# One ring of five PSUM banks for attention and state space model, in place of a ring of three and a ring of two

## The reference

```python
h = layernorm(x) * (1 + ca) + sa
# layer 0, mixer: causal attention and a selective state space model beside each other
xn   = ln(h)
attn = softmax(mask(q @ k.T)) @ v @ o_w          # 16 heads of 8 channels
xz   = xn @ in_proj_w;  x_c = silu(conv4(x_ssm)) # 256 inner channels
dt   = softplus(x_dbc[..., :8] @ dt_w + dt_b)
h_n  = exp(dt * A_n) * h_n + (x_c * dt) * B_n    # n = 0..15, a scan over 512 tokens
y    = sum_n C_n * h_n
ssm  = ((y + x_c * D) * silu(z)) @ ssm_out_w
x1   = h + a * attn + (1 - a) * ssm;  x1 = x1 + gelu(ln(x1) @ w1) @ w2
x    = x + ga * x1
x    = x + gb * moe(layernorm(x) * (1 + cb) + sb)          # 8 experts and a shared one
x    = x + ga1 * band_attention(...)                        # layer 1
x    = x + gb1 * gated_mlp(...)
```

## Time and profile before

| | |
|---|---|
| median of three runs | 1875.94 us (1873.93 to 1879.81) |
| the profiled execution | 1875.14 us |
| its span, first to last instruction | 1873.3 us |
| mean granted TensorE clock | 0.895 |
| busy share of the span | PE 80%, PEld 50%, DVE 72%, ACT 57%, POOL 45% |

### The profile page before, as it was taken

How to read it: one execution, slowest core, us unless ns; L and a number is a source line. 1 busy time by engine, 2 the same in 40 slices (tenths; PEclk the granted TensorE clock), 3 DMA queues, 4 the chain that set the end, 5 groups by cost and what they waited for, 6 DMA issues and landing times. The chain is left out here.

```text
span 1873.3 us, 22056 instructions
## 1 busy us (share of the span) xinstructions
PE 1506.9 (80%) x7196; PEld 935.3 (50%) x7196; DVE 1345.0 (72%) x2025; ACT 1066.2 (57%) x1776; POOL 846.7 (45%) x866
## 2 busy tenths in 40 slices
PE   4757777777777868777776788979999999988778
PEld 3334433434344344343443355558778787844673
DVE  2377868868778687786889167577868686848866
ACT  2555555555555554655555467567787878832107
POOL 3263646656555465554665431112222222336853
PEclk8877898988979989889899989889999999966889
DMA  3121212102122021121210021001111111100001
GB/s 80 51 71 46 65 44 71 57 28 76 54 65 64 27 70 55 45 69 40 67 62 18 1 90 52 24 17 43 45 40 45 40 45 40 51 1 1 1 1 45
DMA packets 61654, 84.72 MB, mean 45 GB/s; under 512 B 6588, under 2 KB 32038, under 8 KB 61542
## 3 DMA queue, kind: packets, MB, share of 16 engines
q1 hardware_dynamic: 61442, 83.30, 14.7%
q10 hardware_dynamic: 100, 0.03, 0.0%
HBM read 74.38 MB, written 8.78 MB: 44 GB/s over the span
## 5 line engine op out<-in xcount | busy, mean ns | idle before, releaser
L1002 PE MATMUL bank<-QK 127*128 127x128 bf16 (+7 forms) x1024 | 252.3, 331 | 126.1 <-DVE Mx L1268 115.1
L1710 POOL TENSOR_TENSOR dBx<-dtx,Bb 128x512 f32<-128x512 f32 x256 | 320.2, 1274 | 5.8 <-DVE hy L1284 5.8
L1317 DVE TENSOR_TENSOR hl<-lsq,hh 128x512 fp32r<-128x512 f32 x320 | 260.9, 826 | 84.2 <-ACT hh L1594 76.2
L1531 ACT ACTIVATE PT<-bank 128x512 f32<-128x512 f32 x320 | 188.2, 595 | 204.8 <-PE bank L1002 203.9
L1284 DVE TENSOR_TENSOR_SCAN hy<-bank,dBx 128x512 f32<-128x512 f32 x256 | 298.1, 1205 | 4.7 <-POOL dBx L1710 4.3
L1268 DVE TENSOR_REDUCE Mx<-bank 128x1 f32<-128x384 f32 (+3 forms) x352 | 217.6, 630 | 88.9 <-PE bank L1002 88.3
L1591 ACT ACTIVATE lsq<-bank,vcol 128x512 f32<-128x512 f32 x320 | 219.1, 693 | 108.0 <-DVE hl L1317 63.2
L1690 POOL TENSOR_SCALAR_AFFINE_SELECT PT<-PT 128x256 f32<-128x256 f32 (+1 forms) x320 | 118.2, 375 | 302.6 <-ACT PT L1531 301.2
L1729 POOL TENSOR_TENSOR stage<-stage,lrs 128x512 f32<-128x512 f32 x64 | 91.7, 1433 | 311.2 <-DVE lrs L1397 311.2
L1002 PEld LDWEIGHTS bank<-QK 127*128 127x128 bf16 (+1 forms) x1024 | 94.3, 106 | 273.3 <-DVE Mx L1268 178.8
L1002 PE MATMUL bank<-x,we1h 128*128 128x512 f32 x640 | 210.8, 411 | 18.8 <-DVE x L1305 9.4
(11 more groups left out here) (255 smaller groups left out, 2475.3 us busy)
## 6 DMA issues: line engine op xcount, KB each, us to landing
Bb<-b_dram SPq DMA_DIRECT2D x128, 256.0 KB, 3.7
stage<-w_rows SPq DMA_DIRECT2D x64, 256.0 KB, 3.2
parts<-part SPq DMA_DIRECT2D x16, 384.0 KB, 2.8
QK<-parts SPq DMA_DIRECT2D x64, 96.0 KB
QK<-parts SPq DMA_DIRECT2D x64, 64.0 KB
stage<-in_L_ffn_We_dram SPq DMA_DIRECT2D x16, 256.0 KB, 3.4
hy<-in_L_attn_x_dram SPq DMA_DIRECT2D x8, 256.0 KB, 5.6
QK<-parts SPq DMA_DIRECT2D x64, 32.0 KB
```

The source lines that it names most:

```text
L1002: return engine.matmul(o, l, r, start=start, stop=stop, tile_position=pos, skip_group_check=True)
L1317: engine.tensor_tensor(hl[:, sl, :], full[:, f, :], hh[:, sl, :].bitcast(F32), ALU.subtract).then_inc(sems["dve_hl"], 1)
L1531: engine.activation(PT[:, it["sl"], :], o[:], ACT.Exp).then_inc(sems["act_exp"], 1)
L1710: engine.tensor_tensor(dBx[:, sl, h], dtx[:, b % 2, h], Bb[:, sl], ALU.mult).then_inc(sems["pool_dbx"], 1)
```

## The change

Attention and state space model take their banks from one ring of five, 0, 1, 2, 6 and 7, each step the next in turn whichever of the two it belongs to. So every step waits for the fifth step before it in the common order to give its bank back. `take2` is gone, and its callers (`branches` for `bx` and `bz`, `steps_of` for `dbc` and `dt`, `accumulate`, `finish` for `yt` and `so`, `taps`) call `take`. While the first norms run, which use banks 0 to 5, the ring is set to 6 and 7 alone. Banks 3, 4 and 5, the order of the steps, and every instruction with its operands' shapes stay as they are; only which bank is written, and so which event is waited for.

```diff
-    ring, ring2 = [0, 1, 2], [0]
+    ring = [0, 1, 2, 6, 7]
...
-    def take2():
-        ring2[0] += 1
-        return 6 + (ring2[0] - 1) % 2
...
-            k = take2()
+            k = take()
             it = step("bx", b=b, h=h, bank=k, free=free.get(f"b{k}"), ready=r_n[b], xc_free=free.get(f"xc{s}"))
...
-            k = take2()
+            k = take()
             it = step("bz", b=b, h=h, bank=k, free=free.get(f"b{k}"), zg_free=free.get(f"zg{s}"))
...
-        k, k2 = take2(), take2()
+        k, k2 = take(), take()
         it = step("dbc", b=b, bank=k, bank2=k2, free=free.get(f"b{k}"), free2=free.get(f"b{k2}"), xc=("act_silu", 2 * b + 1),
...
         for half in range(2):
-            k = take2()
+            k = take()
             it = step("acc", g=g, half=half, bank=k, free=free.get(f"b{k}"), ready=ssm[b]["h", n], bc=ssm[b]["bc"],
...
+    ring[:] = [6, 7]
     run_together(p.norms(first_norms([(1, 1)] + [(b, l) for l in range(2) for b in range(2, NB)])), 12, (mixer, 5, False))
+    ring[:] = [0, 1, 2, 6, 7]
```

## The result

| | before | after |
|---|---|---|
| median | 1874.93 us | 1738.27 us |
| ratio, 95% interval | | 0.9272 (0.9242 to 0.9301) |
| span of the profiled execution | 1873.3 us | 1734.0 us |
| its mean granted clock | 0.895 | 0.934 |

The change takes 136.7 us, 7.3%. I had forecast 58 us and a range down to 1776. The sign and the place were right, the size was not. All times and ratios are of undisturbed executions; one of the ten of the control kernel with the factors in SBUF took 4643 us and is left out, with its profile.

The account below looks back on a forecast made before the run. In the mixers VectorE and TensorE wait for each other in turn, short of banks for look-ahead. The terms 22 + 10 + 26 = 58 us gave 1875 - 58 = 1817 us, range 1776 to 1864.

Parts of the forecast that it names:

- A: In the mixers, dbc no longer waits for the acc just before it to be read out: 22 us gained, bounds 0 and 24.8.
- B: In the mixers, bz, dt and bx no longer wait for the acc directly ahead: 10 us gained, bounds 0 and 27.
- C: In attention's ring, TensorE waits less for row maxima: 26 us gained (46% of 55 us), bounds 0 and 55.
- D: Tighter waits at 227 state space and 107 attention takes: costed at nothing, as the reading engines' order covers them.
- my fourth rival: The clock falls: TensorE's mixer clock goes from 0.88 to 0.80, giving 1858 us; chance 0.04.
- My rival 3: All of it comes back: A, B and C in the mixers at their upper bounds, 107 us, giving 1768 us; chance 0.06.
- the second rival: Slower: attention steps wait for banks an acc holds until VectorE reads it; 1939 us, mild form 1893; chance 0.07.
- The first: Nothing is gained: in the mixers TensorE waits for data instead, or VectorE for other engines; 1870 to 1881 us; chance 0.07.

Follow-up runs that it names:

- the control kernel with the factors in SBUF: The changed kernel, ring of five, with ScalarE writing the scan factors to SBUF instead of banks 4 and 5, and PT at 8 buffers: 1880.48 us, 1.0043.
- The run with spare matmuls: The changed kernel with dbc's old wait put back, plus ten spare matmuls written to dbc's new bank during that wait: 1765.55 us, 0.9461.
- The two runs with spare matmuls: First: ten in dbc's restored wait, 0.9461. Second: the changed kernel with all old waits added, spare matmuls ahead of most takes, 1871.61 us, 1.0017.
- the ring of seven: The control kernel with the factors in SBUF, with banks 4 and 5 added to its ring of five: 1843.49 us, 0.9855.

## Why the prediction was wrong

**What bounds the kernel: right.** The two busiest engines waited for each other for want of banks. With the old waits back the gain is gone (1.0041), and nearly all of it was in the mixers.

**A, `dbc`: right in kind, 22 us taken, 35 measured.** The idle time in the earlier trace rows was 24.8 us, and I held it for the upper bound; the 35, good to 8, are probably above it. VectorE's idle time before `bc` fell from 41.8 to 5.2 us where I expected 17 to stay. I had left the product itself as long as it was, and its matmuls went from 894 to 591 ns. The run with spare matmuls shows this second effect at `bc`, though not in the time.

**B, `bz`, `dt`, `bx`: the step that failed.** I gave 10 of 27.2 us, saying that a scan or maxima already computed would hide the rest. Measured: 40 us, so the cover was not there. This is no effect of the faster surroundings alone: with the attention's waits as before, A and B together still gain 77 us on the kernel before. A wait of TensorE that is not followed at once by one of VectorE was not hidden but carried on: with these waits put back, VectorE waits 27 us more for the maxima behind them. Why it is carried so far, I can only argue: the look-ahead is missing at the next long group, and these steps bring the longest groups of the stretch.

**C, attention: the step that failed.** I gave 26 us, and 59 were measured. I had multiplied by 46%, the share of takes for which the new ring looks further back. Takes are not waits: those 351 held 83% of the waiting, 131 of 158 us. The price of a microsecond of waiting, 36%, was somewhat low as well. It came from 21 us of the trace, and 36% of 131 us is 47 us. That the full 36% of 150.9 us, 55 us, lies so near to 59 is luck, since 27 us of these waits stand at takes that the new ring does not relax.

**D, what becomes tighter: not settled.** I cost it at nothing. 58.6 us of new waits stand before the transposes of `acc`, so the cover that I described was not complete. VectorE waits 3.8 us for these transposes, but by what B teaches that does not make the rest free, and no run has the changed kernel without them. Whatever it is, the 137 us are what is left after it.

**The clock: missing from the sum, and at most a small part of the gain.** It rose, where my fourth rival had it fall. The Trainium skill, "TensorE: Matmul & The Clock Gate", section "A second HAM failure mode: psum-queue depth-cycling", says that TensorE idling in small gaps between bank cycles loses clock. The trace agrees, and it was the kernel before that did so: 0.88 there, 0.95 with fewer gaps. The two runs with spare matmuls raised it and changed the time by no more than their noise; in the second the added work may hide a part of its worth.

**The sum and the range.** 35 + 40 + 59 = 134 us, with 137 measured; the sum closes within the noise of the three prices. The two halves hardly depend on each other: alone on the kernel before, A and B give 77 us (0.9587), attention's part 61 us (0.9672). My rival 3, "all of it comes back", had 107 us because it took the length of the waits as the most for A and B, and 55 us for C. The range ended inside even that. Of the second rival, streams that stop each other, no net loss appeared. The first, waits with new names, is there in the 58.6 us of D, but did not eat the gain.

## What to carry to other kernels

When two in-order streams share an engine, try one ring in the order in which the engine takes from it. Here three shared banks were 0.5% faster than three and two apart, and the other division, two and three, was worse still. Do not take the length of a wait for a buffer as the most that removing it can give. Here both engines at its ends were busy for three quarters of the stretch, and the 62 us by which TensorE's waits for `hy` grew when A and B were put back cost 75 us. And when waits are to be weighted, weight them by where they stand in the trace, not by how many steps of each kind there are.

## What the runs showed of the hardware

A `tensor_tensor_scan` of 128x512 fp32 took 1205 ns with one input in PSUM and the other in SBUF, and 1727 ns on average with both in SBUF. The second figure is a mixture. The least, middle and longest scan, in the ring of seven and then in the changed kernel:

```profile
L1283 DVE TENSOR_TENSOR_SCAN hy<-dec,dBx x256: 1192/1647/2323, 112.4 to 996.5; 128x512 f32<-128x512 f32 x128
```
```profile
L1282 DVE TENSOR_TENSOR_SCAN hy<-bank,dBx x256: 1192/1206/1225, 111.9 to 891.7; 128x512 f32<-128x512 f32 x128
```

Set beside GpSimd's instructions in time, the 18 scans of the ring of seven that none of them overlaps took 1204 ns on average and 1217 at most, with both inputs in SBUF. The 195 that share 0.6 us or more with a `tensor_tensor` of GpSimd took 1857 ns. In the changed kernel 228 scans share as much, and took 1204. So it is not the place of the operand alone that costs, but both inputs in SBUF while GpSimd works there too. GpSimd's products pay as well, 1577 ns in place of 1276.

TensorE's matmuls of 24 columns of weights by 512 of data in fp32 took 591 ns where the granted clock was 1.00, the level of 2.4 GHz, and 1061 at 0.50, that of 1.2 GHz. In the run with `dbc`'s old wait TensorE had been idle for 4.4 us before them, and the clock over the product at 468 us was 0.52. With spare matmuls in the wait the idle time was 1.6 us and the clock 1.00. That saved TensorE some 1.7 us for each product and the kernel next to nothing.
